# Edges of a graph network in two parts: segment sums of part 1 beside the convolution, layer input in DRAM

## The chip, the cores and the metric

The kernel runs on one core of one Trainium2 chip. A core has five engines with instruction queues of their own: TensorE (PE), VectorE (DVE), ScalarE (ACT), GpSimd (POOL) and SyncE (SP), which here only issues DMAs. The metric is the device time of one execution in microseconds. Each queue is worked off in order; engines wait for each other by semaphores that the kernel names.

## What is computed

The graph has 12500 nodes with 128 features and 200000 edges, sorted by their target `dst`. Two layers follow one another, each with a residual sum and a layer norm.

```python
def _round(x, w, b, gamma, beta, src, dst, etype):      # layer 0, twice
    h = relu(_bn(x, gamma, beta))
    h3 = (einsum('nd,od->no', h, w) + b).reshape(N, T, D)
    return segment_sum(h3[src, etype], dst, N)
x = _layernorm(x + (_round(_round(x)) + x))
# layer 1: the convolution, with idx_i = src (the target!), idx_j = dst
h = x @ W_in
W_ij = (ssp(f_ij @ Wf1 + bf1) @ Wf2 + bf2) * f_ij_cutoff
out = segment_sum(h[idx_j] * W_ij, idx_i, N)
x = _layernorm(x + ssp(out @ Wo1 + bo1) @ Wo2 + bo2)
```

In layer 1 the values are read by the sorted index `dst` and summed by the unsorted index `src`. The kernel therefore has to bring the messages into the order of `src` before it can sum them.

## The kernel before, in words

**Sizes.** A tile is 128 edges, a group is 4 tiles (512 edges), a half is 2 groups, an iteration is 2 halves (2048 edges). There are 98 iterations (`ITERS`), 392 groups (`GROUPS`) and 98 blocks of 128 nodes (`BLOCKS`).

**Stages, in order of time.** (1) Batch norm and the table of messages of round 1 (PE L1190 and L1192, DVE L735), then a gather pass: POOL gathers 128 rows per indirect DMA (L459), PE sums a group into its window of 128 nodes by a one-hot matrix (`aggregate`, L1225), DVE adds it to an accumulator. During this pass PE also counts how many edges have their `src` in each block (`count_blocks`). (2) The same for round 2. Before it, `first_places` (L786 to L804) turns the counts into the first place of each block and tile, and into `block_end`; `step_table` (L806) makes from it the table of steps. During the pass `rank_edges` and `pick_ranks` work out for each edge its place in the order of `src` blocks. (3) Layer norm in 25 chunks of 512 nodes: `y_chunk`, `centre`, `scale_rows` on DVE; the normed rows stay in `buf_x`, their product with `W_in` goes to DRAM as `h_in`. (4) The convolution, 98 iterations: PE spreads the window of h onto the edges (L1320), multiplies the attributes (`filter_in`, L1304) and the filter output (L1342, L1346); ACT computes the softplus; DVE makes one-hot matrices (`spread_half`, L974), messages (L1029) and the softplus sum (`soft_half`, L967); POOL scatters each tile of messages with its `src` number, 576 bytes a row, to its place in `sorted_rows` in DRAM (L510). SP refills attributes, ends and windows. (5) The segment sums: the sorted rows come back in groups of 512, and `STEPS` = 392 + 98 - 1 = 489 steps each add one group into one block: a group that reaches over a block's end is loaded once for each block. A step is a load of 288 KB (SP, L413), a one-hot of 128 x 512 (`step_onehot`, DVE L1078), four matmuls (`sum_segment`, PE L1360) and an add into `buf_a` at a column that DVE loads from the step table (`load_columns`, `add_segment`, L1093). Two PSUM banks alternate. (6) The output stage in 25 chunks (PE L1374 to L1385, ACT, DVE L1115 and L1120), the last layer norm, and the stores.

**The order around the change.** Between (4) and (5) stands a full stop: SP waits until all scatters have landed before it loads the first rows, and DVE zeroes `buf_a` (L1070) when the convolution no longer uses it. In the convolution DVE waits before it overwrites a half's messages until the scatters of the half two before have landed (its wait shows at L746), and POOL waits for the messages of each group. PE's order within a half is: spreading of both groups, filter input of the next half, filter output of group 0 and of group 1. The loops are written out by hand; a run-time flag chooses a variant for edges beyond the window, which these inputs don't take.

Of the kernel before, what the change touches and what calls it, by code (L numbers as in the profile page):

```python
# [29 lines left out]
P = 128  # L30
# [3 lines left out]
GROUP_TILES = 4  # L34
# [13 lines left out]
WIDE = 512  # L48
# [12 lines left out]
LOOP2 = (CHUNKS - 1) // 2  # L61
# [4 lines left out]
STEPS = GROUPS + BLOCKS - 1  # L66
STEP_SLOTS = 8
HOT_SLOTS = 4
STEP_LOOPS = (STEPS - 2) // STEP_SLOTS
STEP_COLS = STEPS + 7  # L70

EXP_LN_SET = 6
assert X_COLS * X_PARTS == N and X_COLS % BN_CHUNK == 0 and GROUPS % 4 == 0
assert STEP_COLS <= WIDE and HOT <= WIDE and 2 * LOOP2 == CHUNKS - 1


def gnn_program(nc, dram, out):
# [5 lines left out]
    with ctx:  # L83
# [6 lines left out]
        def sem(name):  # L90
# [4 lines left out]
        htable = nc.dram_tensor("h_in", (NBUF, D), f32).ap()  # L95
        sorted_rows = nc.dram_tensor("sorted_rows", (TILES * P, ROW), f32).ap()
# [45 lines left out]
        first_place = sb("first_place", [P, HOT])  # L142
        block_end = sb("block_end", [P, 1])
        block_end_i = sb("block_end_i", [P, 1], i32)
        beyond_blocks = sb("beyond_blocks", [P, 1])
        window_at = sb("window_at", [P, STEP_COLS])
        step_rows = sb("step_rows", [1, 2, STEP_COLS], i32)
# [8 lines left out]
        bn_raw = first_place[:, 0:N // BN_CHUNK * 6].rearrange("p (c s) -> p c s", s=6)  # L156
# [12 lines left out]
        ones_b = work[:, 10 * WIDE - P // 2:10 * WIDE].bitcast(bf16)  # L169
        place_stage = work[:, SLOTS * TD + 3 * HOT:SLOTS * TD + 3 * HOT + 2 * HALF_TILES].rearrange("p (h t) -> p h t", h=2)  # L170
        rows_in = work[:, 0:STEP_SLOTS * GROUP_TILES * ROW].rearrange("p (q t n) -> p q t n", q=STEP_SLOTS, t=GROUP_TILES)
# [16 lines left out]
        step_hot = onehot[:, :, :, :].rearrange("p h (j t) n -> p (h j) t n", j=2)  # L188
# [6 lines left out]
        block_counts, block_ends = (x_onehot[:, i, 0:HOT] for i in range(2))  # L195
        end_column = x_onehot[:, 2, 0:HIGH]
        step_reached = x_onehot[:, 3, 0:STEP_COLS // 2].bitcast(bf16)
# [13 lines left out]
        ps_steps = ps_b[2][:, 0:STEP_COLS]  # L211
        ps_seg = [ps_b[j][:, 0:P] for j in range(2)]
# [4 lines left out]
        ps_step_iota = ps_b[3][:, 0:P]  # L217
# [32 lines left out]
        s_counts_init, s_reached, s_steps, s_table = (sem(n) for n in (  # L250
            "counts_begun", "steps_reached", "steps_summed", "step_table"))
# [25 lines left out]
        def _(sp):  # L277
# [55 lines left out]

            for m in range(4):
                load_x(m, m)
# [12 lines left out]
            with sp.Fori(0, full) as r:  # L348
                for j in range(4):
                    reload_x(r * 4 + j, j)  # L350
                    store_h(r * 4 + j, j % 2)
            for m in range(4 * full, CHUNKS):
                if m + 7 < CHUNKS:
                    reload_x(m, m % 4)
                if m < CHUNKS - 1:
                    store_h(m, m % 2)

# [11 lines left out]
            for s in range(2):  # L369
                sp.wait_ge(s_hout[s], 16 * (len(range(s, CHUNKS - 1, 2)) + 1))  # L370
            sp.wait_ge(s_hlast, 64)
            for h in range(2):
                load_windows(h, bases[2 * h:2 * h + 2])
            def refill(beyond):
                with sp.Fori(0, ITERS) as r:
# [17 lines left out]

            with sp.If(flag > 0):
                refill(True)
# [9 lines left out]
            def load_steps(k, j, n, used):  # L405

                groups = nc.values_load_multi_w_load_instructions(
                    step_rows[0:1, 0, ds(k, 4)], engines=[mybir.EngineType.SP], min_val=0,
                    max_val=(GROUPS - 1) * GROUP_EDGES, skip_runtime_bounds_check_because="computed from the sorted places")[1]
                for i in range(n):  # L410
                    q = j + i
                    sp.wait_ge(s_seg, used + q)
                    sp.dma_start(rows_in[:, q, :, :].rearrange("p t n -> p (t n)"),  # L413
# [1026 lines left out]
```

## Time and profile before

| | us |
|---|---|
| median of 3 runs | 7002.63 (7001.74 to 7003.13) |
| the profiled execution | 7001.02 |
| its span, first to last instruction | 6999.2 |

| engine | busy us | share of the span |
|---|---|---|
| PE, matmuls | 4673.5 | 67% |
| POOL | 4563.8 | 65% |
| DVE | 3357.9 | 48% |
| ACT | 1147.1 | 16% |

The shares are averages over stages with different limits, so each stage has to be read by itself. The granted clock of PE is 0.722 of full speed over the whole span; it changes between and within the stages. The convolution lies between about 4330 us and 6350 us from the start, the segment sums between 6355 us and 6869 us, and the output stage behind them.

### The profile page before, as it was taken

The numbers are of one execution on the slowest core, as the hardware profiler recorded it, in microseconds if no ns is written. First come the engines' busy times: TensorE is split into PE (matmuls) and PEld (weight loads), VectorE is DVE, ScalarE is ACT, GpSimd is POOL, SyncE is SP. The second block draws the span as 40 slices with busy tenths as digits, with TensorE's granted clock in tenths as the row PEclk, the third lists the DMA queues.
The fourth block names the chain that finished last, engine by engine and source line by source line (L and its number), as shares of the span: only waits on it lengthen the run. The fifth ranks groups of instructions, "written<-read, shape, count | busy, mean of one in ns | idle before, by whom it ended". The sixth has DMA issues, their size and how long they took to land.

```text
span 6999.2 us, 88121 instructions
## 1 busy us (share of the span) xinstructions
PE 4673.5 (67%) x21160; PEld 3339.9 (48%) x21160; DVE 3357.9 (48%) x7881; ACT 1147.1 (16%) x2174; POOL 4563.8 (65%) x4726
## 2 busy tenths in 40 slices
PE   6444444444447566566665667888888888887997
PEld 3333333333334333333333345556555555656884
DVE  6222222222226555555555556444444444447885
ACT  2000000000002000000000003444444444440005
POOL 2777777777772777777777773777777777772000
PEclk9555555555558777777777778777777777788999
DMA  7111111122115111111122124333333333337983
GB/s 266 52 52 52 52 52 52 52 52 52 52 52 204 52 52 52 52 52 52 52 52 52 52 52 111 109 107 108 108 109 108 109 109 109 109 109 220 282 281 102
DMA packets 383980, 666.55 MB, mean 95 GB/s; under 512 B 101455, under 2 KB 177778, under 8 KB 383220
## 3 DMA queue, kind: packets, MB, share of 16 engines
q0 software_dynamic: 151040, 322.50, 15.9%
q1 hardware_dynamic: 232918, 343.81, 15.9%
q8 instruction: 7, 0.11, 0.0%
q14 instruction: 15, 0.12, 0.0%
HBM read 472.56 MB, written 193.35 MB: 95 GB/s over the span
## 4 chain that ended last, share of the span: by engine, by line
POOL 46%; issue 26%; PE 13%; DMA 7%; DVE 4%; DVEq 1%; POOLq 1%; SPq 0%; ACT 0%; ACTq 0%
POOL edge_rows L459 36%; POOL sorted_rows L510 10%; DMA sorted_rows<-edge_rows,idx_stage 6%; PE banks L1360 5%; PE banks L1190 2%; DVE edge_rows L1029 2%; DMA edge_rows<-messages,idx_stage 1%; PE banks L1346 1%; PE banks L1304 1%; PE banks L1225 1%; PE banks L1192 1%; PE banks L1385 0%; PE banks L1342 0%; PE banks L1279 0%; PE banks L1269 0%
## 5 line engine op out<-in xcount | busy, mean ns | idle before, releaser
L459 POOL DMA_INDIRECT edge_rows<-messages,idx_stage x3136 | 2993.9, 955 | 1193.1 <-issue 1031.9
L1225 PE MATMUL banks<-onehot,edge_rows 128*128 128x128 f32 x6272 | 1410.6, 395 | 1798.4 <-DMA edge_rows<-messages,idx_stage 1798.3
L1225 PEld LDWEIGHTS banks<-onehot,edge_rows 128*128 128x128 f32 x6272 | 1203.9, 286 | 2295.5 <-issue 2295.3
L510 POOL DMA_INDIRECT sorted_rows<-edge_rows,idx_stage x1568 | 1533.7, 978 | 491.8 <-issue 429.2
L823 DVE TENSOR_TENSOR buf_a<-buf_a,banks 128x128 f32 x392 | 113.1, 289 | 1373.7 <-PE banks L1225 1373.7
L1304 PE MATMUL banks<-buf_a,wf 33*128 33x512 f32 x788 | 500.3, 765 | 307.6 <-DVE work L967 306.9
L1346 PE MATMUL banks<-wf,work 128*128 128x128 f32 x3136 | 659.0, 376 | 0.0
L1346 PEld LDWEIGHTS banks<-wf,work 128*128 128x128 f32 x3136 | 561.8, 269 | 130.3 <-issue 130.3
L746 DVE COPY idx_stage<-buf_a 128x8 int32 (+1 forms) x196 | 38.5, 196 | 1055.6 <-DMA sorted_rows<-edge_rows,idx_stage 1055.6
L753 DVE TENSOR_TENSOR onehot<-banks,dst_local 128x1024 f32<-128x1024 f32 x394 | 481.6, 1222 | 129.3 <-issue 129.2
L1360 PE MATMUL banks<-onehot,work 128*128 128x128 f32 x3912 | 468.4, 278 | 69.8 <-DVE buf_a L1093 36.5
L1360 PEld LDWEIGHTS banks<-onehot,work 128*128 128x128 f32 x3912 | 448.8, 192 | 89.4 <-DVE onehot L1078 89.1
L1206 PE MATMUL banks<-first_place,ident 128*128 128x392 f32 x784 | 474.0, 700 | 0.0
L1029 DVE SCALAR_TENSOR_TENSOR edge_rows<-banks,buf_a 128x128 f32<-128x128 f32 x1568 | 427.8, 343 | 59.5 <-PE banks L1346 59.4
L1320 PE MATMUL banks<-buf_a,onehot 128*128 128x128 f32 x3136 | 435.9, 299 | 12.5 <-DMA buf_a<-h_in 12.5
L1320 PEld LDWEIGHTS banks<-buf_a,onehot 128*128 128x128 f32 x3136 | 429.2, 219 | 13.3 <-issue 13.3
L1078 DVE SCALAR_TENSOR_TENSOR onehot<-work,window_at,banks 128x512 f32<-128x512 f32 x489 | 362.8, 742 | 82.4 <-PE banks L1360 54.2
L1304 PEld LDWEIGHTS banks<-buf_a,wf 33*128 33x128 f32 x788 | 160.5, 225 | 470.1 <-DVE work L967 401.5
L761 DVE TENSOR_TENSOR work<-banks,src_high 128x784 bf16<-128x784 f32 x394 | 379.4, 963 | 0.0
L823 DVE TENSOR_TENSOR buf_x<-buf_x,banks 128x128 f32 x392 | 112.6, 287 | 538.1 <-PE banks L1225 536.8
L583 ACT ACTIVATE buf_a<-banks 128x512 f32<-128x512 f32 x392 | 234.0, 597 | 760.1 <-DVE edge_rows L1029 472.6
L546 ACT ACTIVATE work<-banks 128x128 f32<-128x128 f32 x100 | 26.2, 277 | 2027.7 <-PE banks L1280 2027.7
(154 smaller groups left out, 4589.9 us busy)
## 6 DMA issues: line engine op xcount, KB each, us to landing
work<-sorted_rows SPq DMA_DIRECT2D x489, 288.0 KB, 3.7
messages<-work SPq DMA_DIRECT2D x196, 320.0 KB, 2.2
buf_a<-dst_rows SPq DMA_DIRECT2D x198, 256.0 KB, 3.5
edge_rows<-messages,idx_stage POOLq DMA_INDIRECT x3136, 2.5
buf_a<-in_attr SPq DMA_DIRECT2D x198, 128.0 KB
buf_a<-h_in SPq DMA_DIRECT2D x396, 64.0 KB
sorted_rows<-edge_rows,idx_stage POOLq DMA_INDIRECT x1568, 2.3
work<-in_xT SPq DMA_DIRECT2D x25, 256.0 KB, 2.7
```

Of the source, the lines that this page charges most:

```text
L459: nc.gpsimd.indirect_dma_start(gathered[:, h, t, :], None, source, bass.IndirectOffsetOnAxis(ap=idx_stage[:, h, t:t + 1], axis=0),).then_i ...
L510: nc.gpsimd.indirect_dma_start(sorted_rows, bass.IndirectOffsetOnAxis(ap=idx_stage[:, h, t:t + 1], axis=0), msg_rows[:, h, t, :], None,).t ...
L753: nc.vector.tensor_tensor(onehot[:, h, :, :], ps_iota.unsqueeze(1).broadcast_to(shape), dst_local[:, ds(it * ITER_TILES + h * HALF_TILES, ...
L761: nc.vector.tensor_tensor(high_hot[:, h, :, :].rearrange("p j (t n) -> p (j t) n", t=GROUP_TILES), ps_iota[:, 0:HIGH].unsqueeze(1).broadca ...
L1029: last = nc.vector.scalar_tensor_tensor(out=msg_rows[:, h, j * GROUP_TILES + t, 0:D], in0=ps_w[j][:, tile], scalar=cut_stage[:, h, j * GRO ...
L1078: nc.vector.scalar_tensor_tensor(out=step_hot[:, q % HOT_SLOTS, :, :], in0=rows_in[:, q, :, D:D + 1].broadcast_to(shape), scalar=window_at ...
L1206: nc.tensor.matmul(ps_places, ident[:, :], first_place[:, :], start=True, stop=False)
L1225: last = nc.tensor.matmul(ps_agg[j], gathered[:, h, j * GROUP_TILES + t, :], onehot[:, h, j * GROUP_TILES + t, :], start=(t == 0), stop=(t ...
L1304: nc.tensor.matmul(ps_z[j], wf1[:, :], f_sb[:, h, j, :], start=True, stop=True).then_inc(s_z, 1)
L1320: last = nc.tensor.matmul(ps_h[j][:, tile], spread[:, h, j * WIDE + t * P:j * WIDE + (t + 1) * P], h_win[:, h, j, :], start=True, stop=True)
L1346: last = nc.tensor.matmul(ps_w[j][:, t * D:(t + 1) * D], soft[:, j, t * P:(t + 1) * P], wf2[:, :], start=False, stop=(t == GROUP_TILES - 1))
L1360: last = nc.tensor.matmul(ps_seg[q % 2], rows_in[:, q, t, 0:D], step_hot[:, q % HOT_SLOTS, t, :], start=(t == 0), stop=(t == GROUP_TILES - 1))
```

## The change

The edges are cut into two parts, each with its own counts, its own first places and its own steps: part 1 is the edges of iterations 0 to 55 (224 groups, 321 steps, padded to 328 with steps that add nothing), part 2 those of iterations 56 to 97 (168 groups, 265 steps). In `sorted_rows` part 2 stands behind part 1.

- The counts of the two parts are kept in two PSUM banks in round 1; `keep_counts` copies both before the batch norm of round 2; `first_places` goes through the chain of scan, difference and block ends once for each part.
- `steps_reached` and `step_table` move from round 2 to the place between the layer norm and the convolution.
- The accumulator of the segment sums is `buf_x` and no longer `buf_a`. So the normed rows of the layer norm are not kept there: `scale_rows` writes them to `x1_stage`, SP stores them to `x1_rows` in DRAM chunk by chunk, and the output stage loads them again, four chunks ahead. `buf_x` is zeroed between the layer norm and the convolution.
- The 41 iterations 57 to 97 of the convolution also do 8 steps of part 1 each (4 in a half), on one PSUM bank. SP waits once for the scatters of iterations 0 to 55 and then issues four row loads at the start of each half.
- The stage behind the convolution does the 265 steps of part 2, in the same loop as before.

```diff
+FIRST_ITERS = 56
+GROUPS_IN = [FIRST_ITERS * GROUP_TILES, GROUPS - FIRST_ITERS * GROUP_TILES]
+STEPS_IN = [g + BLOCKS - 1 for g in GROUPS_IN]
+BESIDE = ITERS - FIRST_ITERS - 1
+FIRST_STEPS = BESIDE * STEP_SLOTS
+STEPS = FIRST_STEPS + STEPS_IN[1]
+STEP_LOOPS = (STEPS_IN[1] - 2) // STEP_SLOTS
...
+            def store_x1(m, s):
+                sp.wait_ge(s_x1, m + (1 + SLOT2))
+                sp.dma_start(x1_rows[ds(m * P, P), :], x1_stage[:, s, :]).then_inc(s_x1out[s], 16)
...
+                def refill_step(r, adding):
+                    bases = load_bases(r + 1)
+                    for h in range(2):
+                        if adding:
+                            load_steps((r - (FIRST_ITERS + 1)) * STEP_SLOTS + 4 * h, 4 * h, 4,
+                                       (r - (FIRST_ITERS + 1)) * STEP_SLOTS + 1)
...
+                with sp.Fori(0, FIRST_ITERS + 1) as r:
+                    refill_step(r, False)
+                sp.wait_ge(s_table, 10)
+                for h in range(2):
+                    for j in range(2):
+                        sp.wait_ge(s_scat[h][j], 64 * FIRST_ITERS)
+                with sp.Fori(FIRST_ITERS + 1, ITERS) as r:
+                    refill_step(r, True)
...
+            def reload_x1(m, q):
+                sp.wait_ge(s_fo, m + (1 + SLOT2))
+                load_x1(m + 4, q)
...
-                nc.vector.tensor_tensor(buf_x[:, ds(m * WIDE, WIDE)].rearrange(blocks, b=4),
+                dve.wait_ge(s_x1out[s], stored)
+                nc.vector.tensor_tensor(x1_stage[:, s, :].rearrange(blocks, b=4),
                                         ps_xrows[s][:, :].rearrange(blocks, b=4), by_row, ALU.mult).then_inc(s_x1, 1)
...
+            def convolution_step(r, first, beyond, adding=False, last_turn=False):
                 for h in range(2):
                     k = r * 2 + h
+                    if adding:
+                        turn = r - (FIRST_ITERS + 1)
+                        columns = load_columns(turn * STEP_SLOTS + 4 * h)
+
+                    def add_step(i):
+                        q = 4 * h + i
+                        n = turn * STEP_SLOTS + q
+                        if not last_turn or q + 2 < STEP_SLOTS:
+                            step_onehot(n + 2, (q + 2) % STEP_SLOTS, turn * 16 + 16 * ((q + 2) // STEP_SLOTS + 1))
+                        add_segment(n, q, columns[i], 0)
 
                     spread_half(r + h, 1 - h)
+                    if adding:
+                        add_step(0)
                     dve.wait_ge(s_hcopy, k * 2 + (2 + SLOT2))
                     stage_cutoff(r + h, 1 - h)
+                    if adding:
+                        add_step(1)
...
                         last.then_inc(s_msg, 1)
+                        if adding:
+                            add_step(2 + j)
                     soft_half(k + 1)
...
+            nc.vector.tensor_copy(ps_step_iota, iota_f[:, 0:P]).then_inc(s_cleared, 1)
+            steps_reached()
+            step_table()
+            dve.wait_ge(s_yc, CHUNKS + SLOT2)
+            dve.wait_ge(s_mean, CHUNKS)
+            nc.vector.memset(buf_x[:, :], 0.0).then_inc(s_cleared, 1)
```

On PE, `sum_segment` of the new loop stands behind the spreading, behind the filter input, and behind each of the two filter outputs:

```diff
+            def sum_segment(k, q, bank):
+
+                pe.wait_ge(s_step_hot, k + 1)
+
+                pe.wait_ge(s_added, k + (1 if bank else 2))
+                for t in range(GROUP_TILES):
+                    last = nc.tensor.matmul(ps_seg[bank], rows_in[:, q, t, 0:D], step_hot[q % HOT_SLOTS][:, t, :],
+                                            start=(t == 0), stop=(t == GROUP_TILES - 1))
+                last.then_inc(s_seg, 1)
...
+                    if adding:
+                        turn = r - (FIRST_ITERS + 1)
+                        sum_segment(turn * STEP_SLOTS + 4 * h, 4 * h, 0)
+                    filter_in(k + 1, 1 - h, (r + h) * 16 + 16)
+                    if adding:
+                        sum_segment(turn * STEP_SLOTS + (4 * h + 1), 4 * h + 1, 0)
...
+                        last.then_inc(s_w, 1)
+                        if adding:
+                            sum_segment(turn * STEP_SLOTS + (4 * h + 2 + j), 4 * h + 2 + j, 0)
```

## Rows read from the trace of the kernel before

**Rows 1.** The page's chain of waits: shares by engine, then by line.

```profile
POOL 46%; issue 26%; PE 13%; DMA 7%; DVE 4%; DVEq 1%; POOLq 1%; SPq 0%; ACT 0%; ACTq 0%
POOL edge_rows L459 36%; POOL sorted_rows L510 10%; DMA sorted_rows<-edge_rows,idx_stage 6%; PE banks L1360 5%; PE banks L1190 2%; DVE edge_rows L1029 2%; DMA edge_rows<-messages,idx_stage 1%; PE banks L1346 1%; PE banks L1304 1%; PE banks L1225 1%; PE banks L1192 1%; PE banks L1385 0%; PE banks L1342 0%; PE banks L1279 0%; PE banks L1269 0%
```

**Rows 2.** Stretches: length; PE, PEld, DVE, ACT, POOL busy; clock; DMA share; GB/s.

```profile
4250.00:4317.00 67.00, 65.90 (x433) 50.55 (x432) 61.05 (x118) 36.21 (x225) 0.00 (x0) 1.00 0.58 165
5100.00:5600.00 500.00, 426.46 (x1852) 285.67 (x1850) 223.49 (x735) 225.59 (x389) 381.07 (x391) 0.75 0.35 109
4600.00:6300.00 1700.00, 1437.52 (x6302) 993.45 (x6302) 747.19 (x2480) 770.61 (x1328) 1296.14 (x1325) 0.77 0.35 109
6500.00:6860.00 360.00, 327.90 (x2754) 314.03 (x2754) 306.68 (x689) 0.00 (x0) 0.00 (x0) 1.00 0.90 282
```

**Rows 3.** Convolution, 5000 to 5900 us: the scatters' group; DVE's wait (sum, times, longest).

```profile
L510 POOL DMA_INDIRECT sorted_rows<-edge_rows,idx_stage x703 | 686.8, 977 | 214.4 <-issue 192.8 <-DVE edge_rows L1029 12.2 <-DVE edge_rows L1023 9.4
...
DVE idx_stage L746 <- DMA sorted_rows<-edge_rows,idx_stage: 463.0, 87, 7.4
```

**Rows 4.** Timeline of eight segment-sum steps: start, us, instruction, idle before.

```profile
6601.90 0.75 DVE L1078 SCALAR_TENSOR_TENSOR onehot<-work,window_at,banks 128x512 f32<-128x512 f32 x1 [0.89 <-PE banks L1360]
6602.56 0.28 DVE L1093 TENSOR_TENSOR buf_a<-buf_a,banks 128x128 f32 x1
6602.76 0.74 DVE L1078 SCALAR_TENSOR_TENSOR onehot<-work,window_at,banks 128x512 f32<-128x512 f32 x1
...
6602.99 7.76 PE L1360 MATMUL banks<-onehot,work 128*128 128x128 f32 x64 [0.62 <-DVE buf_a L1093]
...
6610.27 0.75 DVE L1078 SCALAR_TENSOR_TENSOR onehot<-work,window_at,banks 128x512 f32<-128x512 f32 x1 [0.89 <-PE banks L1360]
```

**Rows 5.** Timeline between convolution and segment sums.

```profile
6337.77 10.72 DVE L1070 MEMSET buf_a<- 128x12800 f32 x1 [2.66 <-issue]
...
6349.13 0.97 POOL L510 DMA_INDIRECT sorted_rows<-edge_rows,idx_stage  x1 [0.30 <-issue]
...
6355.21 1.41 DVE L1078 SCALAR_TENSOR_TENSOR onehot<-work,window_at,banks 128x512 f32<-128x512 f32 x2 [6.71 <-issue]
```

**Rows 6.** Timeline of a convolution half, DVE: messages, softplus sums, one-hots for spreading.

```profile
5071.62 1.12 DVE L1029 SCALAR_TENSOR_TENSOR edge_rows<-banks,buf_a 128x128 f32<-128x128 f32 x4
...
5074.44 1.28 DVE L967 SCALAR_TENSOR_TENSOR work<-banks,work 128x512 f32<-128x512 f32 x2
...
5075.63 1.03 DVE L974 TENSOR_SCALAR onehot<-buf_a,part_f 128x512 f32<-128x512 int16 x2
```

**Rows 7.** Timeline of two convolution halves, PE: one row at low clock, then one half.

```profile
5064.50 3.78 PE L1304 MATMUL banks<-buf_a,wf 33*128 33x512 f32 x4 [3.32 <-DVE work L967]
...
5075.42 1.98 PE L1304 MATMUL banks<-buf_a,wf 33*128 33x512 f32 x4
...
5077.34 0.39 PE L1342 MATMUL banks<-bias_rows,ones_rows 3*128 3x512 bf16 x1
...
5078.74 0.38 PE L1342 MATMUL banks<-bias_rows,ones_rows 3*128 3x512 bf16 x1
...
5080.05 1.95 PE L1320 MATMUL banks<-buf_a,onehot 128*128 128x128 f32 x16
```

**Rows 8.** DMA issues: the row loads of the segment sums, median us to landing.

```profile
work<-sorted_rows SPq DMA_DIRECT2D x489, 288.0 KB, 3.7
```

**Rows 9.** Timeline of the first places: first copy, first scan, last comparison.

```profile
2254.28 0.56 DVE L791 COPY x_onehot<-banks 128x392 f32<-128x392 f32 x1
2254.87 0.97 DVE L792 TENSOR_TENSOR_SCAN x_onehot<-x_onehot 128x392 f32<-128x392 f32 x1
...
2258.34 0.48 DVE L804 TENSOR_SCALAR x_onehot<-iota_f,block_end 128x496 bf16<-128x496 f32 x1
```

**Rows 10.** Timeline of the convolution's start: DVE's first instruction, the first scatter.

```profile
4326.10 0.27 DVE L1043 MEMSET edge_rows<- 128x256 f32 x1 [7.20 <-DMA h_in<-buf_a,last_idx]
...
4338.44 0.96 POOL L510 DMA_INDIRECT sorted_rows<-edge_rows,idx_stage  x1 [13.82 <-DVE edge_rows L1029]
```

More of the change, by code:

```diff
@@ L402, in _ @@
                 sp.wait_ge(s_win_in[h], 32 * (ITERS + 1))
[L405 to L413, printed above, removed]
-                                 sorted_rows[ds(groups[i], GROUP_EDGES), :].rearrange("(p t) n -> p (t n)", p=P)
-                                 ).then_inc(s_step_in[q], 16)
             for h in range(2):
@@ new lines, in load_columns, with add_segment @@
+            def load_columns(k):
+                return nc.values_load_multi_w_load_instructions(
+                    step_column[0:1, ds(k, 4)], engines=[mybir.EngineType.DVE], min_val=0, max_val=NPAD - P,
+                    skip_runtime_bounds_check_because="computed from the sorted places")[1]
+            def add_segment(k, q, column, bank):
+                dve.wait_ge(s_seg, k + (1 + STEP_SLOTS))
+                dve.wait_ge(s_added, k + SLOT2)
+                at = buf_x[:, ds(column, P)]
+                nc.vector.tensor_tensor(at, at, ps_seg[bank], ALU.add).then_inc(s_added, 1)
@@ L1083, in load_columns @@
-            def load_columns(k):
-                return nc.values_load_multi_w_load_instructions(
-                    step_rows[0:1, 1, ds(k, 4)], engines=[mybir.EngineType.DVE], min_val=0, max_val=NPAD - P,
-                    skip_runtime_bounds_check_because="computed from the sorted places")[1]
-            def add_segment(k, q, column):
-                dve.wait_ge(s_seg, k + (1 + STEP_SLOTS))
-                dve.wait_ge(s_added, k + SLOT2)
-                at = buf_a[:, ds(column, P)]
-                nc.vector.tensor_tensor(at, at, ps_seg[q % 2], ALU.add).then_inc(s_added, 1)
@@ L1240, in round_steps @@
             def round_steps(p, beyond):
[L1241 to L1243 removed]
+                for i, (first, end) in enumerate(((0, FIRST_ITERS), (FIRST_ITERS, ITERS))):
+                    if p == 0:
+                        pe.wait_ge(s_hot[0], 1)
+                        nc.tensor.matmul(ps_counts[i], ident[:, :], first_place[:, i, :], start=True, stop=False)
+                    with pe.Fori(first, end) as r:
+                        for h in range(2):
+                            aggregate(p, r, h, i, beyond)
+                    if p == 0:
+                        nc.tensor.matmul(ps_counts[i], ident[:, :], first_place[:, i, :], start=False, stop=True
+                                         ).then_inc(s_closed, 1)
             for rnd in range(2):
@@ new lines, in _ @@
+            pe.wait_ge(s_reached, 2)
+            for i in range(2):
+                n = (FIRST_STEPS, STEPS_IN[1])[i]
+                nc.tensor.matmul(ps_steps[i], ones_b[:, :], step_reached[:, i * FIRST_STEPS:i * FIRST_STEPS + n], start=True,
+                                 stop=True).then_inc(s_steps, 1)
+            def sum_segment(k, q, bank):
[5 more added lines that the diff above has]
+                last.then_inc(s_seg, 1)
```

408 lines of the change are left out of this document (223 added, 185 removed).

## The prediction, as it was written before the changed kernel was run

> **What bounds the kernel now.** I read the chain of waits first: the two gather rounds (L459) hold 36% of it and the scatters (L510) 10%; the last named stage, the segment sums (PE L1360), has 5% [rows 1]. The change moves work out of that last stage into the convolution, so the question is what ends last in each of the two. By the stretches, the convolution has POOL busy for 76% with PE at 85% on a mean clock of 0.75, and the segment sums have no POOL at all, PE 91% and DVE 85% busy at clock 1.00, the level of 2.4 GHz [rows 2]. The groups of the convolution show 703 scatters with 686.8 us busy and 214.4 us of issue before them: (686.8 + 214.4)/703 = 1.282 us each without a real pause, so an iteration of 16 lasts 20.5 us, a half 10.25 us, and POOL sets it. DVE stands waiting for landed scatters 463.0 us in 87 halves, 5.3 us each: that is its room per half [rows 3].
>
> The segment sums: a pair of one-hot and add takes DVE 0.86 us (6601.90 to 6602.76), and 8 steps take 6610.27 - 6601.90 = 8.37 us, of which 0.89 is a pause at the turn of the loop. The 64 PE records of 8 steps span 7.76 us, 0.97 us a step [rows 4]. DVE, with its loads of the column registers, is the bound there, with PE close behind.
>
> **Part by part.** *The last stage gets shorter.* It has 489 steps before and 265 after: 224 fewer, exactly 28 turns of 8. The loop body is the same (two alternating banks, the same shapes). 28 x 8.37 = 234.4 us removed. The zeroing of buf_a (10.72 us at 6337.77) also leaves this place, but it is worth nothing: POOL issues scatters until 6350.1 beside it, and the first one-hot at 6355.21 waits for landed scatters and for the first row loads, which it still does [rows 5].
>
> *The same work goes in beside 41 iterations*, 328 steps, 8 an iteration. Who is late next? POOL keeps its 10.25 us a half. DVE: messages 2 x 1.12, soft 1.28, spread 1.03 and about 0.6 of small copies and handoffs are some 5 us [rows 6]; four pairs add 4 x 0.86 = 3.44 and the column loads about 0.3, with 0.9 at the loop's turn [rows 4]: 9.0 us, below 10.25. PE at the high clock: from the start of the filter input at 5075.42 over the two filter outputs to the start of the spreading at 5080.05 are 4.63 us, the spreading takes 1.95 [rows 7], four segment sums 4 x 0.97 = 3.88 [rows 4]. Sum 10.46 us a half, 20.9 an iteration, just above POOL. So PE becomes the bound, if it gets the high clock: it would be busy nearly without pause, and the stretch that looks like that, the segment sums, has clock 1.00 [rows 2].
>
> Then the order of the two queues. All steps share one bank, so step n's matmuls wait for add n-1, and add n waits for them; both queues are in order. The longest ring runs from a filter output over its messages (1.12), the one-hot (0.67) and add (0.2) to segment sum, spreading, segment sum, filter input, segment sum and the next filter output: 1.99 + 0.97 + 1.95 + 0.97 + 1.92 + 0.97 + 1.40 = 10.2 us and three handoffs of 0.1 to 0.2, 10.6 us [rows 4, 6, 7]. The even halves also have the loop's turn before spread and first add: some 0.3 us of it come out on PE. I take 21.3 us an iteration, 0.8 above POOL's. Bounds: not below 20.5 (POOL still has its 16 scatters); above, 24 (12.0 a half), if each of the four sums is handed over late by 0.35 us. Row loads add no wait in my sum: SP issues the four of a half right after the spreading of the half before; the first lands about 3.7 us after issue [rows 8], 5.5 us after that spreading, and its one-hot comes about 7 us after it.
>
> POOL starts with a lead: the messages of a half lie ready 6.5 us before it turns to them (it has issued 2.3 of 10.25 us of the other half when DVE's wait ends, and DVE needs 1.5) [rows 3, 6]. Used up once, it hides 6.5 us. Cost: 41 x 0.8 - 6.5 = 26 us; bounds 0 and 41 x 3.5 - 6.5 = 137.
>
> *The start of the convolution.* DVE now has, between its last norm chunk and the first messages, ten linked operations of the step tables and the 10.7 us zeroing of buf_x. Linked small operations are 0.2 to 0.6 us each: nine of them took 3.47 us (2254.87 to 2258.34) [rows 9]; with the sums over PE I take 5 us, 15.7 in all. Beside it lie the 7.2 us in which DVE waited for h_in's last rows until 4326.10 [rows 10]: 8.5 us late. The first filter output on PE and messages on DVE follow one another without waiting for the window loads then, which gives about 4 back: first scatter 4 us later than 4338.44 (bounds 0 and 8.5).
>
> *The first places of round 2* have the chain of 3.47 us twice, and two copies of 0.59 instead of one, while the comparison of 0.48 leaves: +3.47 + 0.59 - 0.5 = 3.6 us; the gathers start behind them, so all of it counts [rows 9]. The step table leaves the place before the first aggregation, where the gathers already run ahead: nothing.
>
> *Layer input kept in DRAM.* 25 stores of 256 KB beside 25 loads and 24 stores of the same size. In that stretch DVE is busy for 61.05 of 67 us and DMA 58% at 165 GB/s [rows 2]; half as much again gives about 90%, so DVE stays the bound, with 1.5 us for a late last store (bounds 0 and 8). In the output stage the loads are four chunks ahead and DMA is idle beside them: nothing. Cover gone, a chunk would wait some 3 us once. Counts in two banks cost PE one matmul more: nothing, as it waits for gathers.
>
> *Sum:* -234.4 + 26 + 4 + 3.6 + 1.5 = -199 us. The profiled execution took 7001.0 us (span 6999.2 and 1.8 around it), 1.6 below the median of the runs: 7002.6 - 199 = 6804 us.
>
> **A rule weighed.** The segment sums show clock 1.00 although PE idles 0.6 us at each turn of 8 steps, and the convolution shows 0.75 with pauses of 3.3 us before the filter input [rows 2, 4, 7]. The Trainium skill, TensorE: Matmul & The Clock Gate, section "A second HAM failure mode: psum-queue depth-cycling", says that in a kernel whose groups of matmuls cycle through PSUM banks and wait for them, the clock swings between its two levels. The new loop uses one bank in turns, so by that page the fourth case below holds; the row of the old loop speaks against it.
>
> **The rivals.**
> 1. *POOL stays the bound* (ring and PE fit under 10.25 us, as the separate matmul groups end up closer packed): only the small terms are lost, 7002.6 - 234.4 + 9 = 6777 us. For it: PE's 10.46 is only 0.2 above. Against: the ring leaves nothing over.
> 2. *Handoffs bind*: 12.0 us a half, 24 an iteration; 7002.6 - 234.4 + 9 + 137 = 6914 us. For it: DVE's in-order queue has four waits for PE a half, each behind a one-hot. Against: 1.2 us of DVE's room remain.
> 3. *Row loads come late*: 1.2 MB in one burst beside scatters and windows, at 282 GB/s [rows 2], needs 4.2 us; if each half waits 1.5 us, 82 x 1.5 = 123 us more: 6927 us. For it: SP's queue puts them behind the window loads. Against: DMA's share in the convolution is only 0.35.
> 4. *Slower than before*: PE keeps the convolution's mixed clock. Its 20.9 us at the high level become 20.9/0.77 = 27 us an iteration: 41 x 6.6 = 271 us lost against 225 gained, 7049 us. It decides from 26.0 us an iteration on (41 x 5.5 = 225), that is below a clock of 0.80. All at the low level (the filter input takes 3.78 for 1.98) [rows 7] an iteration would be some 38 us and the time 7500. For it: the convolution's rows now. Against: PE then has no pauses, and a PE without pauses has had the high clock.
> 5. *It doesn't do what it says*: part 1's rows are not all landed when needed, so that SP's one wait for them holds the convolution. That wait is passed once; DVE has the same wait in the same half. At most 10 us: inside the first case.
>
> **Chances.** Forecast 0.55 (its own range 6785 to 6860), rival 1 0.14, rival 2 0.13, rival 3 0.09, rival 4 0.07, others 0.02. The range 6772 to 6905 leaves out rival 4 and the upper ends of 2 and 3. A measurement here tells 0.2% (14 us) from no change; faster 0.91, same 0.01, slower 0.08.
>
> **What would show it.** Right: a last stage of 265 steps at 8.37 us for 8 and some 280 us long; scatters in the 41 iterations with pauses of up to a microsecond a half, PE over 95% busy at clock near 1.00, iterations of 21.0 to 21.6 us; the 57 iterations before them unchanged at 20.5; the first scatter about 4 us later after the norm stage. Wrong: DVE's one-hot waiting for DMA (rival 3), DVE's add waiting for PE with PE idle (rival 2), clock near 0.8 there (rival 4), or no pause on POOL (rival 1). The forecast fails altogether if the 41 iterations take over 26 us.

## The result, and the profile after

The changed kernel takes 6783.73 us (median of 4 runs, 6783.29 to 6784.04), the kernel before 7002.88 us (4 runs beside it): a ratio of 0.9687, 95% interval 0.967 to 0.9704. The forecast was 6804 us with a range from 6772 to 6905. The profiled execution has a span of 6781.5 us, 217.7 less than before.

The page after: busy shares, then the chain of waits by engine and by line.

```profile
PE 4580.0 (68%) x21997; PEld 3326.8 (49%) x21997; DVE 3458.1 (51%) x8106; ACT 1147.2 (17%) x2174; POOL 4567.1 (67%) x4726
...
POOL 44%; issue 24%; PE 21%; DMA 5%; DVE 4%; DVEq 1%; POOLq 0%; SPq 0%; ACT 0%; ACTq 0%
```

Against [rows 1] PE's share of the chain has gone from 13 to 21%, POOL's from 46 to 44%. Whose turn it is where shows in the stretches (length; PE, PEld, DVE, ACT, POOL busy; clock; DMA share; GB/s): norm stage, plain convolution, convolution with sums, last stage.

```profile
4250.00:4330.00 80.00, 74.23 (x462) 56.88 (x462) 67.80 (x133) 38.94 (x230) 1.20 (x1) 0.93 0.74 230
4345.00:5500.00 1155.00, 951.12 (x4296) 669.28 (x4297) 511.54 (x1700) 524.75 (x904) 870.05 (x892) 0.80 0.34 109
5520.00:6300.00 780.00, 779.13 (x5294) 624.30 (x5294) 616.16 (x1741) 349.13 (x601) 595.53 (x606) 1.00 0.70 221
6375.00:6652.00 277.00, 255.22 (x2120) 244.63 (x2120) 234.50 (x530) 0.00 (x0) 0.00 (x0) 0.99 0.90 286
```

In the third row PE is busy for 779 of 780 us at clock 1.00, the level of 2.4 GHz, while POOL has as large a share (0.763) as in the plain stretch before [rows 2]. POOL's group from 5600 to 6200 us (busy, mean ns, idle before) and DVE's two waits there (sum, times, longest):

```profile
L559 POOL DMA_INDIRECT sorted_rows<-edge_rows,idx_stage x466 | 459.0, 985 | 142.1 <-issue 142.1
```

```profile
DVE buf_x L1108 <- PE banks L1419: 66.6, 58, 1.2
DVE edge_rows L1145 <- PE banks L1467: 55.5, 116, 0.7
```

(459.0 + 142.1)/466 = 1.290 us a scatter, 10.3 us a half, and no idle time but issue. In [rows 3] it was 1.282, with some waits for DVE among it. DVE's wait for landed scatters, 5.3 us a half in [rows 3], is gone; 2.1 us a half of waits for PE are left. One half of the new loop (start, us, instruction, idle before), PE and four DVE rows (L1403 filter input, L1419 segment sum, L1463 and L1467 filter output, L1433 spreading; L1145 messages, L1093 one-hot, L1108 add):

```profile
5702.42 1.98 PE L1403 MATMUL banks<-buf_a,wf 33*128 33x512 f32 x4
...
5704.33 1.16 PE L1419 MATMUL banks<-work,buf_a 128*128 128x128 f32 x8
...
5705.42 0.39 PE L1463 MATMUL banks<-bias_rows,ones_rows 3*128 3x512 bf16 x1
5705.63 0.29 DVE L1108 TENSOR_TENSOR buf_x<-buf_x,banks 128x128 f32 x1 [1.15 <-PE banks L1419]
...
5706.73 1.06 PE L1419 MATMUL banks<-work,buf_a 128*128 128x128 f32 x8
5706.93 1.13 DVE L1145 SCALAR_TENSOR_TENSOR edge_rows<-banks,buf_a 128x128 f32<-128x128 f32 x4 [0.56 <-PE banks L1467]
...
5707.98 0.74 DVE L1093 SCALAR_TENSOR_TENSOR work<-buf_a,dst_local,banks 128x512 f32<-128x512 f32 x1
...
5708.63 0.28 DVE L1108 TENSOR_TENSOR buf_x<-buf_x,banks 128x128 f32 x1
...
5709.03 1.10 PE L1419 MATMUL banks<-work,buf_a 128*128 128x128 f32 x8
...
5709.96 1.95 PE L1433 MATMUL banks<-buf_a,onehot 128*128 128x128 f32 x16
...
5712.74 1.12 PE L1403 MATMUL banks<-buf_a,wf 33*128 33x512 f32 x2
```

From one filter input to the next are 5712.74 - 5702.42 = 10.32 us, and none of PE's rows has an idle time before it.

Where the 217.7 us come from, by marks that both traces have:

| stretch | before | after | difference | forecast |
|---|---|---|---|---|
| start to the first gather of round 2 | 2259.84 | 2269.90 | +10.1 | +3.6 |
| to the end of the norm stage on DVE (difference only) | | | +0.6 | +1.5 |
| to the first scatter at 4338.44 and 4358.10 (difference only) | | | +9.0 | +4 |
| first to last scatter | 2010.7 | 2012.0 | +1.3 | +26 |
| last scatter to last add | 519.7 | 281.9 | -237.8 | -234.4 |
| last add to the end | 130.4 | 129.5 | -0.9 | 0 |

The +1.3 from the first to the last scatter is a difference of two larger ones. From the first scatter of iteration 57 to the first of iteration 97, the 40 full turns that carry the sums, it is 825.3 us (5525.59 to 6350.89) against 820.5 before: +4.8. The 56 plain iterations ahead of them took 1146.7 us against 1150.5: -3.8, with the same loop. Why the plain loop differs by that much the traces don't say.

### The profile page after: what moved, and what is told of

Its sections match the earlier page's. It is cut to its first block, busy times and chain, and to the rows that moved or that the text cites. A ratio compares the mean times of both kernels' runs of the same rounds, so it can differ in the third digit from the quotient of the medians.

```text
span 6781.5 us, 90856 instructions
## 1 busy us (share of the span) xinstructions
PE 4580.0 (68%) x21997; PEld 3326.8 (49%) x21997; DVE 3458.1 (51%) x8106; ACT 1147.2 (17%) x2174; POOL 4567.1 (67%) x4726
## 4 chain that ended last, share of the span: by engine, by line
POOL 44%; issue 24%; PE 21%; DMA 5%; DVE 4%; DVEq 1%; POOLq 0%; SPq 0%; ACT 0%; ACTq 0%
POOL edge_rows L508 37%; PE banks L1419 8%; POOL sorted_rows L559 7%; DMA sorted_rows<-edge_rows,idx_stage 4%; PE banks L1467 3%; PE banks L1287 3%; PE banks L1403 2%; PE banks L1433 2%; DVE edge_rows L1145 2%; DMA edge_rows<-messages,idx_stage 1%; PE banks L1463 1%; PE banks L1322 1%; PE banks L1289 1%; PE banks L1507 0%; PE banks L1378 0%
## 5 line engine op out<-in xcount | busy, mean ns | idle before, releaser
L1419 PE MATMUL banks<-work,buf_a 128*128 128x128 f32 x4744 | 614.5, 280 | 41.4 <-DVE work L1093 20.8
L1419 PEld LDWEIGHTS banks<-work,buf_a 128*128 128x128 f32 x4744 | 563.8, 193 | 115.2 <-DVE buf_x L1108 63.2
L1467 PE MATMUL banks<-wf,work 128*128 128x128 f32 x3136 | 574.7, 339 | 0.0
L1403 PE MATMUL banks<-buf_a,wf 33*128 33x512 f32 x788 | 424.0, 661 | 204.8 <-DVE work L1047 204.2
L1467 PEld LDWEIGHTS banks<-wf,work 128*128 128x128 f32 x3136 | 483.7, 235 | 112.2 <-issue 112.2
L1145 DVE SCALAR_TENSOR_TENSOR edge_rows<-banks,buf_a 128x128 f32<-128x128 f32 x1568 | 431.2, 344 | 86.4 <-PE banks L1467 86.4
L1093 DVE SCALAR_TENSOR_TENSOR work<-buf_a,dst_local,banks 128x512 f32<-128x512 f32 x593 | 438.7, 740 | 55.0 <-PE banks L1419 24.6
L1433 PE MATMUL banks<-buf_a,onehot 128*128 128x128 f32 x3136 | 419.8, 291 | 9.1 <-DMA buf_a<-h_in 9.1
L1433 PEld LDWEIGHTS banks<-buf_a,onehot 128*128 128x128 f32 x3136 | 411.1, 211 | 9.6 <-issue 9.6
```

What stands on the lines that cost most here:

```text
L1093: nc.vector.scalar_tensor_tensor(out=step_hot[q % HOT_SLOTS], in0=rows_in[:, q, :, D:D + 1].broadcast_to(shape), scalar=window_at[:, ds(k, ...
L1145: last = nc.vector.scalar_tensor_tensor(out=msg_rows[:, h, j * GROUP_TILES + t, 0:D], in0=ps_w[j][:, tile], scalar=cut_stage[:, h, j * GRO ...
L1403: nc.tensor.matmul(ps_z[j], wf1[:, :], f_sb[:, h, j, :], start=True, stop=True).then_inc(s_z, 1)
L1419: last = nc.tensor.matmul(ps_seg[bank], rows_in[:, q, t, 0:D], step_hot[q % HOT_SLOTS][:, t, :], start=(t == 0), stop=(t == GROUP_TILES - 1))
L1433: last = nc.tensor.matmul(ps_h[j][:, tile], spread[:, h, j * WIDE + t * P:j * WIDE + (t + 1) * P], h_win[:, h, j, :], start=True, stop=True)
L1467: last = nc.tensor.matmul(ps_w[j][:, t * D:(t + 1) * D], soft[:, j, t * P:(t + 1) * P], wf2[:, :], start=False, stop=(t == GROUP_TILES - 1))
```

## Experiments

The first four ran beside a kernel before of 7005.43 us; where they are compared with the changed kernel, 2.5 us of a difference can be the difference between the two measurements.

**What do the sums cost where they stand now?** Part 1's 328 steps are left out.

```diff
-                convolution_step(ITERS - 1, False, beyond, True, True)
+                convolution_step(ITERS - 1, False, beyond)
```
(and the same for the loop before it, on PE and in the row loads; part 2's counts start from zero)

> Leaves part 1's 328 steps out (their row loads, one-hots, matmuls and adds; part 1 is missing from the sums), so that the 41 iterations are plain convolution. It measures what the steps cost there. Theory now: POOL sets the pace in both kernels (1.290 us a scatter beside the sums, 1.28 without) and the sums lie wholly beside it; only the 1.3 us by which the stretch from the first to the last scatter grew come back: -1 to -3 us, clock of the stretch back from 1.00 to about 0.8. Rival, the prediction's term: the sums cost 0.8 us an iteration less a lead of 6.5: -26 us.

Measured: 6791.12 us, 7.4 slower than the changed kernel. First to last scatter took 2009.0 us, 3.0 less. In the 40 turns that carried the sums it is 6.9 less (818.4 for 825.3 us); the 56 plain iterations took 4.2 more (1150.9 us). So the sums cost 3 us by the whole stretch and 7 us by their own turns, 0.17 us an iteration and not 0.8. The time was lost elsewhere: from the last scatter to the last add it took 291.6 us instead of 281.9, at the same 265 steps. The stretches beside the convolution (5600 to 6200 us) and in the last stage:

```profile
5600.00:6200.00 600.00, 482.88 (x2231) 346.29 (x2230) 263.11 (x885) 272.46 (x470) 456.65 (x470) 0.82 0.35 109
6375.00:6652.00 277.00, 247.25 (x2070) 236.87 (x2070) 231.74 (x519) 0.00 (x0) 0.00 (x0) 1.00 0.89 277
```

Without the sums PE is busy for 80% at clock 0.82; with them for 100% at 1.00. The 3.9 us of matmuls a half found their place in the idle time and in the higher clock. The last stage runs at 277 GB/s instead of 286. Why it does, with the same instructions, the traces don't say; other paces come back below.

**Is PE at its limit?** One of a half's four segment sums is done twice.

```diff
+                for t in range(GROUP_TILES if bank == 0 and q % 4 in EXTRA_SUMS else 0):
+                    nc.tensor.matmul(ps_seg[bank], rows_in[:, q, t, 0:D], step_hot[q % HOT_SLOTS][:, t, :],
+                                     start=(t == 0), stop=(t == GROUP_TILES - 1))
```

> One segment sum of each half is done twice on PE (4 more matmuls, some 0.95 us a half at the high clock; same result). Theory now: PE runs without a pause beside the sums, 10.32 us a half against POOL's 10.26, so it becomes the bound at once: 82 x (10.32 + 0.95 - 10.26) less 2.9 us of lead left = +80 us, POOL with pauses of about 1 us a half. Rival 1: PE's records only look full, and POOL's pace still holds: +0 to +5 us. Rival 2: the ring over DVE is the bound and the group lies beside it: +0 to +20 us.

Measured: 6854.61 us, 70.9 more; first to last scatter 2083.0 us, +71.0. Stretch and POOL's group from 5600 to 6200 us:

```profile
5600.00:6200.00 600.00, 600.00 (x4175) 489.62 (x4174) 446.16 (x1230) 248.48 (x428) 414.72 (x429) 1.00 0.64 204
```

```profile
L560 POOL DMA_INDIRECT sorted_rows<-edge_rows,idx_stage x429 | 414.8, 967 | 185.6 <-issue 110.1 <-DVE edge_rows L1146 61.7 <-DVE edge_rows L1140 13.7
```

A half takes 600/429 x 8 = 11.19 us, 0.87 more, and POOL now waits for DVE. PE is full: nearly every added matmul shows in the time. Both rivals fall.

**How much room has DVE?** Each one-hot of a half is built twice.

```diff
+                if more and q % 4 in EXTRA_HOTS:
+                    nc.vector.scalar_tensor_tensor(
+                        out=x_onehot[:, :, (q % 4) * P:(q % 4 + 1) * P], in0=rows_in[:, q, :, D:D + 1].broadcast_to(shape),
+                        ...
```

> Each of the four one-hots of a half is built twice on DVE (4 x 0.67 = 2.7 us a half more, the spare ones to an unused place). Theory now: DVE has 8.15 us of work in 10.32 us, so 2.15 us of room a half; 10.85 us of work exceed it by 0.53: 82 x 0.6 less 2.9 us of lead = +46 us, up to +90 if the ring's handoffs keep a wait of 0.5 us a half. Rival, the prediction's ring of 10.6 us a half over DVE and PE: the four lie in it, 10.6 + 2.7 = 13.3 us a half: +240 us. Rival 2: POOL's pace covers it, +0 to +5 us.

Measured: 6913.84 us, 130.1 more; first to last scatter 2135.6 us, +123.6. My number was too low by a factor of over two, and the rival's ring of 13.3 us a half falls too: the half took 600/403 x 8 = 11.9 us.

```profile
5600.00:6200.00 600.00, 559.66 (x3527) 440.00 (x3527) 541.96 (x1364) 235.09 (x405) 397.95 (x403) 0.95 0.62 194
```

```profile
DVE edge_rows L1152 <- PE banks L1474: 52.5, 57, 1.8
PE banks L1426 <- DVE buf_x L1114: 40.1, 94, 0.5
```

DVE works 10.8 us of it and waits 1.1 for PE; PE waits 0.8 for DVE's adds. Where it waits shows in the rows (messages, the spare one-hot, the one-hot, the add, the segment sum):

```profile
5700.56 1.12 DVE L1152 SCALAR_TENSOR_TENSOR edge_rows<-banks,buf_a 128x128 f32<-128x128 f32 x4 [0.71 <-PE banks L1474]
...
5701.60 0.73 DVE L1095 SCALAR_TENSOR_TENSOR x_onehot<-buf_a,dst_local,banks 128x512 f32<-128x512 f32 x1
...
5702.26 0.74 DVE L1099 SCALAR_TENSOR_TENSOR work<-buf_a,dst_local,banks 128x512 f32<-128x512 f32 x1
...
5702.92 0.28 DVE L1114 TENSOR_TENSOR buf_x<-buf_x,banks 128x128 f32 x1
...
5703.25 1.16 PE L1426 MATMUL banks<-work,buf_a 128*128 128x128 f32 x8 [0.43 <-DVE buf_x L1114]
```

The one-hots are for later steps, but in DVE's queue they stand between the messages and the add, and PE waits for the add. The ring that sets the pace here runs from the add behind the spreading (ended 5709.40) over a segment sum and a filter output on PE to the messages at 5712.06 and then, without idle time on DVE, to the same add a half later (ended 5720.90): 11.50 us. Three of the four spare one-hots lie in it, 2.0 us, so without them it is about 9.5 us. It is not the ring that the prediction drew, which holds one one-hot and would have grown by 0.66 us only; so this run says nothing against the 10.6 us of that one. The changed kernel itself does: its half takes 10.32 us.

**Does the clock hang on PE's full queue?** Every second segment sum has one matmul instead of four (the other rows are missing from the sums).

```diff
+                tiles = 1 if bank == 0 and q % 2 else GROUP_TILES
```

> Every second segment sum beside the convolution has one matmul instead of four (three quarters of its rows are missing from the sums): PE has some 1.45 us a half less work, 8.9 of 10.26 us at the high clock. Theory now: POOL's pace holds, -1 to +1 us, and the clock tells whether PE's full queue is what kept it at 1.00: I expect 0.9 to 1.0. Rival: with pauses of 1.4 us a half the clock falls to the plain convolution's 0.8, 8.9 us become 11.1, and fewer matmuls make the kernel slower: +60 to +70 us.

Measured: 6783.49 us, no change. The stretch from 5600 to 6200 us:

```profile
5600.00:6200.00 600.00, 569.95 (x3382) 433.04 (x3381) 472.86 (x1342) 271.99 (x469) 457.64 (x468) 0.95 0.71 223
```

PE has less to do, the clock goes down to 0.95, and 95% of the time is still filled. The 40 turns took 823.2 us, 2 less than in the changed kernel: POOL nearly holds its pace. The rival's +60 us doesn't come.

**Three repairs, and another kind of chip.** The next four runs met a chip where the kernel before took 8425.5 us, 20% more than on the first. The three after them (all three repairs again, the changed kernel again, two spare one-hots) met one with 8287.51 us, and the last run one with 8408.28 us.

The first three edits each take one small cost out; the fourth kernel has all of them.

*Zeroing and tables out of the convolution's start:*

```diff
-            step_table()
...
-            nc.vector.memset(buf_x[:, :], 0.0).then_inc(s_cleared, 1)
...
+                    if clearing and h == 0:
+                        nc.vector.tensor_scalar(buf_x[:, ds((r - 1) * WIDE, WIDE)], iota_f[:, :], 0.0, None,
+                                                ALU.mult).then_inc(s_cleared, 1)
```
(`step_table()` stands behind iteration 0 now)

> The zeroing of buf_x goes into 25 pieces of 512 columns, one in each of iterations 1 to 25, and the step tables behind iteration 0; nothing is left out. It measures what these two cost ahead of the first messages. Theory now: the own delay of the first scatter there, 9.0 us against the kernel before, comes back: -9 us, and the pieces and the tables lie in DVE's room of 5.3 us a half: 0. Rival, the prediction's term for that place: -4 us. Rival 2: the pieces (0.55 us each) or the tables show in POOL's pace: +2 to +10 us over the first.

*Indices ahead of the first places:*

```diff
+            dve.wait_ge(s_clear[1], 1)
+            for h in range(2):
+                stage_indices(1, 0, h)
             first_places()
```

> The gather indices of round 2 are staged on DVE ahead of the first places instead of behind them, so POOL's first gather no longer waits for that chain. Theory now: the chain of first places took 6.9 us (4.6 in the kernel before) and all of it lies on the path: -7 us. Rival: PE, which still waits for the chain, then holds the gathers' buffers once and gives it back: -2 to 0 us.

*Count copies behind the batch norm's statistics:*

```diff
-            keep_counts()
             batch_norm(1, buf_a)
+            keep_counts()
```
(and PE waits for both copies before it starts the products of round 2)

> The two copies of the block counts on DVE go behind the batch norm's statistics. Theory now: they took 3.0 us for 2 x 0.56 because POOL's zeroing of buf_x runs at that moment and DVE's copy waits for it to end (both end together in the trace); behind the statistics they lie beside PE's and ACT's first block: -2.5 to -3 us. Rival: the statistics are held by the same zeroing, since they come next: -1 to 0 us.

*All three, on each of the three chips:*

> The three edits together, nothing left out. They lie in three places one behind the other on the path, so they add up: -9 - 7 - 2.5 = -18 us against the changed kernel, about 6765 us. Rival: one shadows another: -10 us.

> The three edits together once more (zeroing and tables out of the convolution's start, gather indices first, count copies later), since the first four were measured on a chip on which both the kernel before and all of these are over 20% slower. Theory: -9, -7 and -2.5 us in their three places against the changed kernel on the same chip, -18 us in all; each place is read by itself from the trace (first gather of round 2 at 2260 instead of 2269.9; first scatter at 4329 to 4332 instead of 4358.1; from there to the last scatter 2012). Rival: the 25 pieces or the tables show in POOL's pace, or PE's wait for the first places takes the place of the gathers' wait: -10 us in all.

> The three edits together (zeroing and tables out of the convolution's start, gather indices ahead of the first places, count copies behind the statistics), on whichever chip it falls. On one like the first: -9, -7 and -2.5 us in their places against the changed kernel, 6765 us and a ratio to before of 0.966; rival 6774 us (one takes the place of another). On one like the two slow ones: 1.015 to 1.023 of before, where the three edits drown in pauses of some 6 us that the engines make there.

*The changed kernel itself on such a chip:*

> The changed kernel itself, on the chip of this call, as the measure for the others. If this chip is like the first one: ratio to before 0.969. If it is like the second one, on which variants of it took 1.022 to 1.024 of before: over 1.01, which would say that the change loses on such a chip and not that its variants do.

Measured, with the kernel before on the same chip, the two intervals that the repairs aim at (start of POOL's zeroing to the first gather of round 2; last gather to first scatter), and the last stage:

| kernel | us | before there | ratio | zeroing to gather | gather to scatter | last stage |
|---|---|---|---|---|---|---|
| before, first chip | 7002.88 | | 1 | 139.9 | 103.7 | 519.7 |
| changed, first chip | 6783.73 | 7002.88 | 0.9687 | 146.3 | 112.4 | 281.9 |
| changed, second kind | 8436.80 | 8287.51 | 1.0172 | 146.2 | 114.3 | 280.4 |
| start repaired | 8627.70 | 8425.5 | 1.0234 | 145.8 | 108.1 | 287.4 |
| indices first | 8614.96 | 8425.5 | 1.0218 | 141.2 | 110.9 | 281.6 |
| counts later | 8625.28 | 8425.5 | 1.0237 | 143.6 | 111.3 | 281.5 |
| all three | 8613.01 | 8425.5 | 1.0221 | 140.3 | 104.3 | 287.4 |
| all three, again | 8429.95 | 8287.51 | 1.0169 | 139.5 | 104.2 | 289.1 |
| all three, third | 8595.43 | 8408.28 | 1.022 | 139.8 | 104.3 | 288.6 |

The changed kernel did not run on the chip of the first four, so each of the single edits is read beside those of its neighbours that leave its interval alone. Indices first: 141.2 against 145.8, -4.6 (forecast -7). Counts later: 143.6, -2.2 (-2.5 to -3). Start repaired: 108.1 against 110.9 and 111.3, some -3, where the forecast was -9. DVE does reach its first instruction of the convolution (the zeroing in [rows 10]) 11 us sooner behind the norm stage, 9.0 instead of the 19.9 us of "indices first"; but then it waits 5.30 us instead of 2.97 before the first messages for the filter output on PE, and 3 us are left. All three together, beside the changed kernel on the same chip: -6.7 (-9.5) and -10.1 (-9). So the third fell short alone and not with the others; the same interval takes 110.9 to 114.3 us in kernels that don't touch it. But in all four runs with the start repaired the last stage takes 6 to 9 us longer than in the others on such chips, as it took longer without the sums, and the totals of repaired and changed kernel, 8429.95 (8419.52 to 8441.54) and 8436.80 (8418.40 to 8443.18), can't be told apart. No repaired kernel ran on the first kind of chip. That the combined version beats the changed kernel is not shown.

The larger finding is in the third row of the table: on the second kind of chip the change itself loses, 1.0172 (1.0158 to 1.0186). The stretches of the plain and of the adding loop there:

```profile
5300.00:6500.00 1200.00, 953.77 (x3494) 653.10 (x3494) 415.57 (x1375) 405.39 (x736) 718.64 (x736) 0.66 0.27 85
6800.00:7800.00 1000.00, 717.78 (x3955) 577.20 (x3955) 472.33 (x1299) 254.50 (x448) 440.48 (x450) 0.79 0.41 129
```

An iteration of 16 scatters takes 1200/736 x 16 = 26.1 us in the one and 1000/450 x 16 = 35.6 us in the other, where the first chip has 20.5 and 20.6. As an estimate, 41 x 9.5 = 390 us are lost against the 238 that the last stage gives: 152 us, and 149 were measured. (It takes the plain loop's 26.1 us for the kernel before; that kernel has no trace on such a chip.) The lost time stands in pauses of about 6 us on DVE, one in each half of the adding loop, with PE's sum long ready:

```profile
7019.41 0.74 DVE L1093 SCALAR_TENSOR_TENSOR work<-buf_a,dst_local,banks 128x512 f32<-128x512 f32 x1
7025.80 0.29 DVE L1108 TENSOR_TENSOR buf_x<-buf_x,banks 128x128 f32 x1 [5.65 <-remote]
```

The waits of that loop (6800 to 7800 us, 56 halves):

```profile
POOL sorted_rows L559 <- DVE edge_rows L1145: 438.6, 57, 8.6
DVE buf_x L1108 <- remote: 301.0, 54, 6.6
...
PE banks L1419 <- DVE buf_x L1108: 247.2, 47, 6.1
```

"remote" means that no event of this core explains the wait. In the plain loop such pauses come once an iteration (46 on DVE in 46 iterations), on the first chip not at all. Each stops DVE, then PE, then POOL. A half takes 17.6 us here instead of 10.3, of which DVE's pauses are 5.6; no engine's work bounds the loop, and the last experiment agrees.

**Two spare one-hots instead of four:**

> Two of the four one-hots of a half are built twice on DVE (1.35 us a half more). With four the half took 11.83 us; if all of them lie in the ring over DVE and PE, the ring without them is 11.83 - 2.65 = 9.2 us, and two make it 10.5: 82 x (10.5 - 10.26) less 2.9 us of lead = +17 us against the changed kernel. Rival 1, the prediction's ring of 10.6 us a half, 11.95 with two: +135 us. Rival 2, DVE's room of 2.15 us a half counts whole: 0.

Measured: 8402.68 us, 34 less than the changed kernel beside it; first to last scatter 2903.1 us against 2923.4. On this chip more work on DVE made the kernel faster, so it says nothing on the ring; it says that the pauses don't depend on the amount of DVE's work alone. What they are was not shown.

## Why the prediction was right, and where it was not

The number came out well, on the kind of chip that it was made for; its likeliest case did not. Rival 1 came closest: POOL shows no pause, 6777 us against 6783.7. My own case had a range from 6785 up. Part of the good number is luck: the errors of the terms have both signs, and on the other kind of chip the forecast would have failed altogether.

- *The last stage, -234.4:* right. 224 steps went; the other 3.4 us of the measured -237.8 are a better pace, 8.25 us for eight steps instead of 8.37 (272.4 us for 264 steps between the adds at 6379.6 and 6652.0).
- *The sums beside the convolution, +26:* the step that failed. Measured +1.3 over the whole convolution and +4.8 in the turns that carry the sums (6.9 against the first experiment). PE's sum was right (10.46 forecast, 10.32 measured, busy without pause, clock 1.00). Mis-sized was the ring of 10.6, and with it the 21.3 us an iteration that I took from it. The rows of the half above give its terms: 8.02 us on PE from the segment sum at 5709.03 over spreading and filter input to the end of the next filter output (5706.73 + 10.32 = 5717.05), 2.18 us on DVE from the end of a filter output (5706.73) over the messages and the one-hot to the end of the add (5708.91), and 0.05 us from an add to the matmul that waits for it (5703.20 to 5703.25 in the third experiment). That is 10.25 us. The terms themselves were near, 10.17 without handoffs; what was too much is the 0.4 us for three handoffs, where two cost 0.25, and 0.16 on PE. So the ring lies just below PE's own 10.32. (DVE's terms in the prediction add up to 9.6 us and not 9.0; DVE was busy for 8.15 us a half, and nothing hangs on it.)

  The lead of 6.5 us that was to hide a part is not used up bit by bit. Ahead of the new loop a half's first messages lay ready 7.6 us before POOL turned to them; in the first half with sums it is 3.2 us (5522.4 and 5525.6), and in the last it is 3.2 us still (6358.0 and 6361.2). POOL's own half has grown to the same 10.32 us: in 79 of the 80 halves one scatter takes over 1.05 us instead of 0.97, before in 30 of 80. Which of the two, POOL with that scatter or PE without a pause, sets the 10.32 us isn't shown. The second experiment says that PE has some 0.1 us a half left, the fourth that with less work on PE only 2 us in all come back.
- *The start of the convolution, +4:* measured +9.0. The tables took 6 us and not 5, and the zeroing costs more than its row:

```profile
4335.40 0.06 DVE L887 MEMSET dst_local<- 128x7 f32 x1
4338.19 10.72 DVE L1163 MEMSET buf_x<- 128x12800 f32 x1 [2.73 <-DMA h_in<-buf_a,last_idx]
4348.92 0.27 DVE L1168 MEMSET edge_rows<- 128x256 f32 x1
```

  The 2.73 us ahead of it seem to belong to it: [rows 5] has 2.66 before the same instruction, and the store of h_in that the row names is waited for only behind the zeroing in the code. With them it costs 13.4 us. Against [rows 10] the last row comes 22.8 us later, 12.2 of them made here; 3.2 come back by the first scatter.
- *The first places, +3.6:* measured +10.1. The chain itself grew by 2.4. What I had not counted: the two copies of the counts on DVE stand beside POOL's zeroing of buf_x,

```profile
2123.56 10.78 POOL L539 MEMSET buf_x<- 128x12800 f32 x1
...
2130.36 4.02 DVE L795 COPY idx_stage<-msg_idx 128x8 int32 x1
2131.99 3.00 DVE L839 COPY x_onehot<-banks 128x392 f32<-128x392 f32 x2
2135.03 5.33 DVE L766 BATCH_NORM_STATS2 first_place<-buf_a 128x6 f32<-128x500 f32 x9
```

  where the small copy ends 0.04 us and the two others 0.65 us after the zeroing does; [Rows 9] had one of them in 0.56. The Trainium skill, "SBUF — State Buffer", section "Who interferes with whom", says that a DVE copy in a two-port mode and a GpSimd instruction exclude each other for the whole instruction; the small copy agrees, which ends with the zeroing here and on the second chip. The two others read PSUM, and why they are held as well is not shown; behind the statistics both take 1.17 us, and the gathers start 2.2 to 2.6 us sooner. The rest is a round 1 that ended 3.6 us later (it starts 0.9 later, and POOL has one pause of 1.75 us in it) and a message stage 1.0 longer.
- *Layer input in DRAM, +1.5:* +0.6, at 230 GB/s and a DMA share of 0.74. Output stage 0: -0.9.

The sum was wrong by 18.4 us because 24.7 on the sums was too much and 11.5 on the two small places too little; the last stage, the norm stage and the end make up the other 5.2.

The rule that was weighed, the Trainium skill's "TensorE: Matmul & The Clock Gate", section "A second HAM failure mode: psum-queue depth-cycling", gives no fall of the clock here: it speaks of groups with short idle times of PE between them, and the loop with one bank in turns had none and clock 1.00; with six of the sums' sixteen matmuls a half gone it was still 0.95. Of the rivals, handoffs at 12 us a half, late row loads and a mixed clock show nowhere on the first chip. Rival 4's deciding point of 26 us an iteration was passed on the second kind of chip, by another mechanism than the one named.

## What to carry to other kernels

Where two in-order queues take turns on one bank, draw the ring in the order of the queues: what is built two steps ahead lies in it all the same if it stands between the two instructions that the ring passes. Then size the handoffs from rows, one for each change of the engine: here a ring that was 0.35 us a half too long made 26 us out of 5. PE with clock 0.75 and 85% busy had more room here than 15%, since the added work brought the clock with it; busy for 100% at clock 1.00 it had none. Small work put on the path between two stages deserves the same care as the large loop: here it cost 19 us and was forecast at 8. A small difference over a long stretch can be two larger ones: split it at the marks where the code changes. And a gain measured on one chip is the gain on that chip.

## What the hardware showed unexpectedly

- One program, unchanged, took 7003 and 7005 us in two measurements and 8288, 8408 and 8426 us on three other chips, within 0.3% on each. Single instructions last as long (gather 955 to 958 ns, scatter 967 to 971 ns); added are pauses of some 6 us that no event explains. The plain loop meets one an iteration, the adding loop two, and with two spare instructions a half in its body it took 34 us less.
- The zeroing of 12,800 columns on DVE is shown with 10.72 us and costs 13.4 with the idle time ahead of it; on POOL 10.78 us are shown.
- The loop of the last stage has several paces with the same instructions: over its last 240 steps eight take 8.20 us in the changed kernel, 8.30 with the spare one-hots, 8.32 before, 8.40 with the start repaired and 8.49 without the sums (DMA at 286 GB/s in the first, 277 in the last). The changed kernel has 8.20 on both kinds of chip. Which one a kernel gets goes with edits far ahead of it.
- A scatter on POOL takes 1.11 us instead of 0.97 beside DVE's one-hots for spreading (5712.53 beside 5712.33); one such in each half makes 1.290 of 1.282 us a scatter.
